# Convolution of a recurrent layer's output: zero products removed, decays formed on ScalarE, a ring of eight tile buffers over three memory areas

## What is computed

```python
x = x + _L0_attn_ref(_L0_cond_ref(x, cond, Wx, Wh, b), A_log, D, C_re, C_im, log_dt)

# _L0_cond_ref: next_h = tanh(x_t @ Wx + b + prev_h @ Wh), step by step, 512 steps
# _L0_attn_ref:
dt = jnp.exp(log_dt); A = -jnp.exp(A_log)                       # 256 features, 64 states
at = dt[:, None, None] * A[None, None, :] * t[None, :, None]
K = jnp.einsum('mn,mln->ml', C_re, jnp.exp(at))                 # one kernel per feature
y = irfft(rfft(u) * rfft(K))[..., :L]                           # causal convolution over time
return y.transpose(0, 2, 1) + u * D
```

## Time and profile before

| | |
|---|---|
| median of three runs | 1241.49 us (1240.78 to 1248.24) |
| the profiled execution's own time | 1247.86 us |
| its span | 1246.1 us |
| PE busy | 1168.6 us, 94% of the span |
| DVE, ACT, POOL busy | 605.3, 538.9, 333.9 us |
| DMA | 89.53 MB in 85342 packets, mean 72 GB/s |
| clock that TensorE was granted, mean | 0.967 |
| L475 MATMUL, zero products of all shapes, x521 | 143.6 us busy |
| arena<-k_pad, DMAs of 256 KB, x64 | 6.4 us median to landing |

### The profile page before, as it was taken

One profiled execution on the slowest core, in us unless ns is written; L12 is line 12 of the kernel. 1 busy time (PEld: TensorE's weight loads), 2 busy tenths in 40 slices (PEclk: granted clock), 3 DMA queues, 4 the chain that ended last, 5 costly groups with the idle time before them and its releaser, 6 DMA issues. The chain is left out here.

```text
span 1246.1 us, 63053 instructions
## 1 busy us (share of the span) xinstructions
PE 1168.6 (94%) x26393; PEld 850.2 (68%) x26408; DVE 605.3 (49%) x1989; ACT 538.9 (43%) x1824; POOL 333.9 (27%) x324
## 2 busy tenths in 40 slices
PE   8999999999999999988989898789997999999994
PEld 4666666666666666654544455457777999999993
DVE  2333333333333333354653999977455555556551
ACT  2333333333333333353444755633324656566652
POOL 3111111101111111115640005536200255544554
PEclk9999999999999999998998987979998999999997
DMA  2111111113320000017861001104122466666643
GB/s 78 46 68 68 63 62 68 68 68 57 40 28 9 8 7 9 9 32 152 167 125 36 1 0 69 48 25 154 59 86 87 119 136 154 146 132 137 141 71 43
DMA packets 85342, 89.53 MB, mean 72 GB/s; under 512 B 8658, under 2 KB 71655, under 8 KB 85299
## 3 DMA queue, kind: packets, MB, share of 16 engines
q1 hardware_dynamic: 70706, 71.86, 21.6%
q0 software_dynamic: 14592, 17.10, 8.3%
HBM read 56.82 MB, written 33.96 MB: 73 GB/s over the span
## 5 line engine op out<-in xcount | busy, mean ns | idle before, releaser
L1087 DVE STREAM_TRANSPOSE zt<-ps 128x32 f32<-128x32 f32 x1024 | 160.8, 195 | 357.2 <-PE ps L512 357.2
L831 ACT ACTIVATE hring<-zt 128x8 f32<-128x8 f32 x1024 | 159.7, 201 | 343.3 <-DVE zt L1087 322.3
L492 PE MATMUL ps<-wx,xst 128*8 128x64 f32 x8320 | 219.6, 223 | 0.0
L512 PE MATMUL ps<-wh,hring 128*8 128x64 f32 x8192 | 215.3, 222 | 0.1
L512 PEld LDWEIGHTS ps<-wh,hring 128*8 128x8 f32 x8192 | 119.2, 88 | 62.6 <-issue 2.7
L456 POOL DMA_INDIRECT out<-arena,dest x80 | 127.5, 1594 | 118.8 <-ACT arena L978 96.6
L495 PE MATMUL ps<-brow,tri 1*8 1x64 f32 x4160 | 155.0, 219 | 0.0
L492 PEld LDWEIGHTS ps<-wx,xst 128*8 128x8 f32 x8320 | 147.1, 91 | 3.7 <-issue 2.3
L475 PE MATMUL ps<-zero 128*128 128x256 bf16 (+2 forms) x521 | 143.6, 278 | 3.6 <-DVE ps L1062 3.6
L779 PE MATMUL ps<-xgT_hi,ew_hi 128*128 128x320 f32 (+1 forms) x384 | 119.8, 312 | 2.2 <-DVE xgT_lo L1333 2.2
L779 PE MATMUL ps<-xgT_hi,ew_lo 128*128 128x320 f32 (+1 forms) x384 | 120.0, 312 | 0.0
(11 more groups left out here) (190 smaller groups left out, 1970.6 us busy)
## 6 DMA issues: line engine op xcount, KB each, us to landing
arena<-k_pad SPq DMA_DIRECT2D x64, 256.0 KB, 6.4
slots_in<-mid SPq DMA_DIRECT2D x16, 645.0 KB, 3.3
mid<-slots_in SPq DMA_DIRECT2D x16, 645.0 KB, 4.3
arena<-in_ex_down SPq DMA_DIRECT2D x16, 384.0 KB
arena<-in_ex_gate SPq DMA_DIRECT2D x16, 352.0 KB
arena<-in_ex_up SPq DMA_DIRECT2D x16, 352.0 KB
xst<-in_x_steps SPq DMA_DIRECT2D x66, 64.0 KB, 1.8
xtok<-in_x_tok SPq DMA_DIRECT2D x16, 256.0 KB, 2.7
```

Source lines behind the costliest of these rows:

```text
L492: nc.tensor.matmul(sums_at(bank, t)[Q * j:Q * j + B], xst[:, bank, k, t], wx[:, k, j * W:(j + 1) * W], start=t < 2 and k == 0, stop=False, ...
L512: last = nc.tensor.matmul(sums_at(bank, t)[Q * j:Q * j + B], hring[:, (n - 1) % (2 * G), k], wh[:, k, j * W:(j + 1) * W], start=False, sto ...
L831: nc.scalar.activation(hring[:, n, k], zt[:, n % 2, k * Q:k * Q + B], ACT.Tanh).then_inc(s_h, 1)
L1087: nc.vector.transpose(zt[:, n % 2, k * Q:(k + 1) * Q], sums_at(bank, t)[:, k * Q:(k + 1) * Q]).then_inc(s_zt, 1)
```

## The change

- `keep_up` is no longer called in the convolution (own_block, carried, by_time). The recurrence keeps it.
- The 192 columns of own_block become two matmuls, 128 columns from a tile buffer and 64 from a buffer `pw` of the powers, so each group has eight matmuls in place of four.
- `decay_args` on POOL goes. `decays` on ACT forms exp(dta * iota_t) by itself: eight instructions of 128x128 with dta as a per-partition scale in place of one of 128x1024 over POOL's product. The table iota_t now holds negative numbers.
- `power_args(s)` on POOL waits for s_xc of chunk s-2 (DVE's carry is done) in place of s_tmm.
- The tiles have eight slots: two in arena, two in mid, and four in big, the area that held u before it was turned. Each slot has its semaphore. Chunks 0 to 3 are loaded during the recurrence; chunks 4 to 7 are issued once u is turned (s_utr), chunks 8 to 15 when own_block of chunk s-8 has signalled s_tmm.
- The loops over the chunks are written out on all engines.

The diff, cut to its core:

```diff
@@ buffers @@
-        tp = part(0, [2, CG, J, P + NST])
+        tiles = [w.rearrange("p (g j t) -> p g j t", g=CG, j=J) for v in (arena[:, 0:4096], mid[:, 2584:6680], big[:, :])
+                 for w in (v[:, n:n + CG * J * P] for n in range(0, v.shape[1], CG * J * P))]
+        NSLOT = len(tiles)
+        pairs = [v.rearrange("p (z g n) -> p z g n", z=2, g=CG) for v in (arena[:, 0:4096], mid[:, 2584:6680])]
+        pw = part(4096, [2, CG * J, NST])
...
@@ SyncE @@
-            def toeplitz(z, chunk):
+            def toeplitz(s):
                 for g in range(CG):
-                    sp.dma_start(tp[:, z, g, :, 0:P], kt[:, :, bass.ds(chunk * CG + g, 1), :].rearrange("p j o t -> p j (o t)")).then_inc(s_t0[z], 16)
+                    sp.dma_start(tiles[s % NSLOT][:, g], kt[:, :, CG * s + g, :]).then_inc(s_tile[s % NSLOT], 16)
...
+            sp.wait_ge(s_utr, 2 * C * TB)
+            for s in range(4, NSLOT):
+                toeplitz(s)
             sp.wait_ge(s_kst, 16 + 16 * KG * IT)
-            with sp.Fori(1, NCH // 2) as i:
-                for z in range(2):
-                    sp.wait_ge(s_tmm, 2 * i + z - 1)
-                    toeplitz(z, 2 * i + z)
+            for s in range(NSLOT, NCH):
+                sp.wait_ge(s_tmm, s - NSLOT + 1)
+                toeplitz(s)
@@ GpSimd @@
-            def conv_args(s, z):
+            for s in range(2, NCH):
                 pool.wait_ge(s_zero, 1)
-                pool.wait_ge(s_tmm, s + 1)
-                power_args(z, s + 2)
-                pool.wait_ge(s_zero, 1)
-                pool.wait_ge(s_qmm, 2 * s + 2)
-                decay_args(z, s + 2, s_qa)
...
+                pool.wait_ge(s_xc, s - 1)
+                power_args(s)
@@ TensorE, own_block @@
                     for j in range(J):
-                        last = nc.tensor.matmul(ps[Q * j:Q * j + Q, 2 * z + g // 2, o:o + P + NST], ust[:, z, g, j], tp[:, z, g, j],
-                                                start=g % 2 == 0, stop=False, skip_group_check=True, tile_position=(0, Q * j))
-                    if g < CG - 1:
-                        keep_up(128)
+                        nc.tensor.matmul(ps[Q * j:Q * j + Q, 2 * z + g // 2, o:o + P], ust[:, z, g, j], tiles[s % NSLOT][:, g, j],
+                                         start=g % 2 == 0, stop=False, skip_group_check=True, tile_position=(0, Q * j))
+                    for j in range(J):
+                        last = nc.tensor.matmul(ps[Q * j:Q * j + Q, 2 * z + g // 2, o + P:o + P + NST], ust[:, z, g, j], pw[:, z, J * g + j],
+                                                start=False, stop=False, skip_group_check=True, tile_position=(0, Q * j))
                 last.then_inc(s_tmm, 1)
-                keep_up(128)
...
@@ ScalarE @@
-            def decays(s, z):
-                act.wait_ge(s_qa, s + 1)
-                nc.scalar.activation(qx[:, z], qx[:, z], ACT.Exp, scale=-1.0).then_inc(s_qe, 1)
+            def decays(s):
+                for g in range(CG):
+                    for h in range(NH):
+                        last = nc.scalar.activation(qx[:, s % 2, NH * g + h], iota_t[:], ACT.Exp, scale=dta_q[:, CG * s + g, h:h + 1])
+                last.then_inc(s_qe, 1)
```

More of the change, by code:

```diff
@@ L230, in build @@
         s_late = sem("s_late")
-        s_t0 = [sem("s_t00"), sem("s_t01")]
+        s_tile = [sem("s_tile%d" % n) for n in range(NSLOT)]
         s_yst = [sem("s_yst0"), sem("s_yst1")]
@@ L392, in _ @@
             pool.wait_ge(s_dtm, 4)
[L393 to L396, removed]
+            for s in range(2):
+                power_args(s)
             zeros = zero[:, 0:C * G * B].rearrange("p (k t b) -> p k t b", k=C, b=B)
@@ L584, in by_time @@
                 last.then_inc(s_ytr, 1)
-                keep_up(512)
             pe.wait_ge(s_uev, 8)
             pe.wait_ge(s_uea, 8)
-            own_block(0, 0, False)
-            own_block(1, 1, False)
-            carried(0, 0)
-            for s in (2, 3):
-                own_block(s, s % 2, True)
-                carried(s - 1, 1 - s % 2)
-                by_time(s - 2, s % 2, False)
-            with pe.Fori(2, NCH // 2) as i:
-                for z in range(2):
-                    own_block(2 * i + z, z, True)
-                    carried(2 * i + z - 1, 1 - z)
-                    by_time(2 * i + z - 2, z, True)
-            carried(NCH - 1, 1)
-            by_time(NCH - 2, 0, True)
-            by_time(NCH - 1, 1, True)
+            for s in range(NCH + 2):
+                if s < NCH:
+                    own_block(s)
+                if 1 <= s < NCH + 1:
+                    carried(s - 1)
+                if s >= 2:
+                    by_time(s - 2)
             def x1_turned(b):
@@ L1126, in _ @@
             dve.wait_ge(s_x, 16 * PIECES)
-            PER = 5
-            base = chain[0]
-            for z in range(2):
-                states(z, z)
             for s in range(2):
-                carry(s, s)
-                states(s, s + 2)
-            assert chain[0] == base + 2 * PER
-            with dve.Fori(1, NCH // 2 - 1) as i:
-                chain[0] = i * (2 * PER) + base
-                for z in range(2):
-                    carry(2 * i + z, z)
-                    states(z, 2 * i + z + 2)
-                    add_x(2 * i + z - 2, z)
-            chain[0] = base + PER * (NCH - 2)
-            for z in range(2):
-                carry(NCH - 2 + z, z)
-                add_x(NCH - 4 + z, z)
-            for z in range(2):
-                add_x(NCH - 2 + z, z)
+                states(s)
+            for s in range(NCH + 2):
+                if s < NCH:
+                    carry(s)
+                if s + 2 < NCH:
+                    states(s + 2)
+                if s >= 2:
+                    add_x(s - 2)
             zeros = zero[:]
```

112 lines of the change are left out of this document (54 added, 58 removed).

## The result

The changed kernel takes 1236.77 us in the median of 15 runs (1228.11 to 1244.17), the kernel before 1245.71 us in 15 runs beside them (1237.27 to 1249.16). The ratio is 0.9937, 95% interval 0.9909 to 0.9965. So the gain is 0.6%, some 8 us by the ratio and 8.9 by the medians, and not the 29 us of the forecast. The direction was right, and the time lies above the range.

What follows compares the result with a forecast made beforehand. The convolution was bound by PE's 6.08 us a chunk and two-slot tiles, then by the tile stream. Ending at 632.3 instead of 661.45 us gains 29.2: 1241.5 - 29.2 = 1212.3 us, range 1201 to 1226.

Steps and rivals of the forecast that it cites:

- Written-out loops cost nothing by themselves: Convolution on PE: 264 load and matmul instructions a chunk, written out, were to add no time.
- PE's chunk: Convolution: PE's work 4.1 us a chunk in place of 6.08; 4.3 with the ring of hand-overs between engines.
- The reckoning by rounds: PE's matmuls, four side by side: 0.12 us a round of 128 columns, 0.06 a round of 64.
- ACT's term: ACT in the convolution: eight decays 1.6 to 2.3 us in place of 1.06, sum 3.5 to 4.2 a chunk, hidden.
- The tile stream: Tile DMAs of chunks 4 to 15: queue always full, 5.9 us a chunk, chunk 15 landing at 623.4 us.
- PE waiting for k_pad DMAs from about chunk 9 on: Sign of a right forecast: PE waits for tiles in the later chunks, which come 5.9 us apart.
- The tail: From own_block(15) to the convolution's end: 8.9 us in place of 12.3.
- The loss is worth nothing in itself: POOL in the convolution: losing 1.90 us of work a chunk gains nothing, since POOL had 2.32 us of slack.
- the later wait: POOL's wait moved from s_tmm to s_xc, 2.3 us later; adds nothing in the steady state.
- Rival 2: Convolution: the clock falls where PE waits for tiles, from chunk 9 on; 13.5 us lost, 1226 us; chance 0.10.
- the four rivals: Convolution: stream not the bound (0.18), clock falls at waits (0.10), clock low from the start (0.04), stream at 6.85 us (0.12).
- The other side: Convolution: without filler the lower clock holds from the start, ending 11.6 us later, 1253 us; a rival, chance 0.04.

Runs made afterwards that it cites:

- ring4: The changed kernel with four tile buffers in big for chunks 4 to 15, PE's program still written out; 1240.57 us, before 1240.91.
- ring4_loop: ring4 with PE's program for chunks 4 to 15 as a loop of three turns of four chunks; ratio to before 0.9845.
- few_tiles: The changed kernel with the tiles of chunks 8 to 15 not loaded, PE's program the same; 1211.48 us, before 1240.91.
- loop_merged: The changed kernel with PE's loop from chunk 2 on, four buffers in arena and mid, own_block's 192 columns in one matmul; ratio to before 0.9800.
- few_pool: few_tiles with the decays' product back on POOL and one Exp over it on ACT; 1219.16 us, before 1239.24.
- before_nofill: The kernel before without keep_up in the convolution, nothing else changed; ratio to before 0.9963.
- with_fill: The changed kernel with keep_up called in the convolution as before; 1247.3 us, before 1244.97.
- nofill_act: before_nofill with the change's decays on ACT and POOL's wait moved to s_xc; ratio to before 0.9954.
- before_written: The kernel before with only PE's loop over chunks 4 to 15 written out; 1253.15 us, before 1244.97.
- loop_early: The changed kernel with PE's loop (three turns of four chunks) from chunk 2 on, four buffers in arena and mid; ratio to before 0.9788.

## Why the prediction failed, point by point

- **The size of the gain** was off: 29.2 us forecast, some 8 measured, 1236.8 us where the range ended at 1226. (4.2 us of the distance are the base: the forecast started from three runs of the kernel before, 1241.5 us, and the fifteen beside the result had 1245.7.) The step that failed is the last sentence of the working: "Written-out loops cost nothing by themselves: PE now has 264 load and matmul instructions a chunk". I had counted the instructions and looked for waits in a place of the old trace where they had time to arrive. ring4 against ring4_loop puts the price at 17.3 us of stage in one profiled execution each. In the kernel after it is up to 27.1 us of direct waits, 23.4 of them inside a step, and 7.0 us of rows at the lower clock, against few_tiles. The page of before had the hint, the row of q8 with 27 pieces, and I had not read it.
- **PE's chunk**: 4.1 to 4.3 us forecast, 4.18 measured wherever the program arrives in time (after from 631 us on, few_tiles). The reckoning by rounds held. ACT's term did not: its eight decays took 2.44 us (few_tiles, 586.21), above the 1.6 to 2.3 of the forecast. Over seven such chunks (586.15 to 615.41 us) ACT was busy 28.18 us and PE 27.96 of 29.26, so ACT was as full as PE; that less work on PE alone would not help there is likely, and not tested.
- **The tile stream**: 5.9 us a chunk forecast; SP issued at 5.9 and the last tiles came in time. Issue to landing rose from 6.6 to 7.2 us. "PE waiting for k_pad DMAs from about chunk 9 on" did not appear in after, because PE had become slower than the stream. It appears in loop_merged, where most of the program is out of the way, and its stage of 86.7 us is near my 82.3, 4.1 us of issue included. The tail was forecast at 8.9 us and took 9.25 in after (648.30 to 657.55).
- **own_block(2)** was to start at 557.2, 7.2 us behind the first. It starts at 560.5, 7.9 us behind the first, its carried(0) broken by a 1.5 us wait for the program.
- **The decays and POOL**: "The loss is worth nothing in itself" was wrong as a term. It was judged from POOL's own slack, and the cost lies on DVE: 1.1 us a chunk (few_pool). It did not hurt the sum, since the change removes that product. A forecast for the filler's removal alone would have been too good, as before_nofill was. The price of "the later wait", nothing, held.
- **Rival 2, the clock.** The clock did fall in the stage, to 0.90 in the mean, but as a follower: behind the waits for the program, not from waits for tiles, and not for want of filler (with_fill). Its mechanism is real all the same: nofill_act shows the lower clock behind waits for tiles. The remark that the trace agrees for the 3.79 us gap only was wrong by the prediction's own rows, where the gap of 1.92 us was followed by it too. None of the four rivals was the case that came.
- **The other side** (slower than before) did not come. But the written-out program with four buffers, ring4, stood in its one run where the kernel before stands (1240.57 against 1240.91 us).

The Trainium skill, "Runtime: NRT & Kernel Launch", section "Instruction fetch mechanics", has each engine's instructions brought in blocks of 16 KiB, 256 instructions, by a DMA queue of its own while the current block runs, and calls the cost "mostly hidden". The pieces of 16 KB are seen here. Hidden they are in few_tiles behind the stream and in before_written; under the stream at 184 GB/s they are not. The section also holds that a taken branch can break the fetching and that kernels prefer full unrolling. Here it is the loop that is cheaper: a body of four chunks, 1056 instructions, repeated without a new piece in 37 us of ring4_loop.

## What to carry to other kernels

TensorE's program is a DMA load too (the other engines' programs were not tested). Before a loop is written out, divide the some 250 instructions of a piece (16 x 264/17 here) by the engine's rate, and ask whether a piece can come in that time beside the transfers that run there; if the answer is close, keep a loop whose body repeats, and make the ring of buffers fit the body. Waits put down to issue in the middle of a step, where no semaphore stands, and the count of the instruction queue on the page, are the signs. And when filler or another delay goes, look at what it kept apart: two engines that took turns may now meet.

## What the hardware showed that was not expected

- Under a full tile stream (184 GB/s, 512 B packets) PE got one 16 KB piece of program in 7.5 us; without the stream it took one in 3.75 us with no wait seen. A wait cost up to 7.0 us (ring4).
- A DVE multiplication or addition with both operands in SBUF that meets a product on POOL lasts until that product ends: 0.27 us becomes 1.16 to 1.82. DVE's instructions with an operand in PSUM kept their 0.43 us. The copy of u in states, with one operand in SBUF, was slower too in before_nofill, 785 ns in the mean against 421 before. The Trainium skill, "GPSIMD Engine Reference", section "Specifications", says that POOL shares its SBUF interfaces with DVE, with contention for DVE instructions in a 2-port mode or with two SBUF inputs. The rows agree for two inputs; whether the copy in states runs in such a mode, no run shows.
- The filler that was kept for the clock cost 13.4 us of stage in with_fill (one execution) and did not hold the clock (0.93), while without it, in few_tiles and loop_early, the clock was 0.96.
